# Keys first in self attention, roundings three steps later in cross attention

## The chip, the cores and the metric

The kernel runs on one core of a Trainium2 chip. The metric is the time of one execution on the device in microseconds; lower is better. The core has five engines that run their own instruction streams in order: PE (TensorE), DVE (VectorE), ACT (ScalarE), POOL (GpSimd) and SP (SyncE, which only issues DMA transfers here). They meet at semaphores: an instruction may wait until a semaphore has reached a count, and whatever stands behind it on its engine waits too.

## The reference

Two transformer layers over x (16 batches of 56 tokens, width 256) with a context ctx (16 batches of 1500 tokens, width 256). The change touches the attention part of the second layer:

```python
ln_out = _ln(hidden_states, ln_w, ln_b)
q  = _ln(_fp8_linear_pertensor(ln_out, wq, ...).reshape(b, s, g, hpg, d), qln_w, qln_b)
k  = _ln(_fp8_linear_pertensor(ln_out, wk, ...).reshape(b, s, g, d), kln_w, kln_b)
v  = _fp8_linear_pertensor(ln_out, wv, ...).reshape(b, s, g, d)
core = _gqa(q, k, v)                       # self attention, 56 keys
qx = _ln(_fp8_linear_pertensor(ln_out, wqx, ...), qxln_w, qxln_b)
kx, vx = split(einsum('bsi,oi->bso', cond, w_kv_x))
xout = _gqa(qx, _ln(kx, kxln_w, kxln_b), vx)   # cross attention, 1500 keys
catq = _div_clamp_fp8(concatenate([core, xout]), proj_smooth)
```

There are 16 query heads and 8 key heads of 128 channels. `_div_clamp_fp8` divides, clips to 448 and rounds to bfloat16 and then to fp8.

## The kernel before

Seven stages run one after the other, each with its own block of the five streams: context statistics, attention and experts of the first layer, `self_attention`, `cross_attention`, projection and experts of the second layer. Two of them change.

**`self_attention`** (L727) works on 8 pairs of batches; a pair's 112 tokens lie on the partitions. Its projections are cut into 12 chunks of four heads: queries 0 to 3, queries of cross attention 4 to 7, keys 8 and 9, values 10 and 11 (`KIND`, L716). A turn of a pair has 12 slots, one for each chunk, and each engine's `turn` is a list of what it does in slot t. A chunk is projected by PE (L1016, two slots ahead), squared on ACT (L900), summed on DVE (L1127), made a standard deviation on ACT (L906), normalised on DVE (L1134, L1136), transposed by PE (L1027) and copied by ACT (L933). The attention of the pair before runs in the same slots, at places given by tables (L778 to L780): `SCORES` on PE (L1037, L1040), `MAXIMA` on DVE (L1142, L1146), `EXPS` on ACT, `SUMS` on DVE and POOL, `TURNED` (transposes) and `VALUES` on PE, `OUTPUT` (rounding on DVE L1158 to L1164, then POOL L869, L874). `SCALED` and `QUANTISED` say in which slots the inputs of the next two pairs are rounded. PE's projection takes one of three PSUM banks, so it waits for the normalisation three chunks back.

**`cross_attention`** (L1217) runs over 32 units, two (h = 0, 1) for each batch b, four key heads each; a unit has 6 steps of two context tiles of 125 tokens. Step i of unit u on each engine:
- PE: scores of unit u (L1468, 24 one-pass products of high and low parts), then small work of older units, then the values of the step ten back (L1505, 24 products). The small work: step 0 transposes of the maxima (L1514), step 1 and 2 the folding of the next unit's queries (L1445), step 2 spreading the maximum (L1475) and the sums of the exponentials of unit u-2 (L1528), step 4 spreading their reciprocals (L1480), step 5 the value projection (L1489).
- DVE: scores times scale (L1556), minus the maximum (L1574), low part of the exponentials (L1580), running maximum (L1593, L1598), and for unit u-3 in step 0 the scaled result ca (L1561) and its rounding cb, ce, cc (L1602 to L1606).
- ACT: exponential (L1422), high part (L1427), in step 3 the diagonal of reciprocals (L1404) and the copy ut (L1410), in step 4 rsc (L1417).
- POOL: sum of the exponentials (L1355, L1358, L1361), low part of the context (L1366, in steps 1, 3 and 5 of h = 1), and the end of the rounding of unit u-3 (L1370, L1374), which writes `cat`.
- SP: its queue of one batch is shown below. `load_ct(b, c)` brings chunk c (of three) of the transposed context's high and low parts, which PE needs from step 2c of the first unit of b on (L1459). `store` waits for `cat_ready`.

```python
for c in range(NCH):
    load_cn(b, c)
if more:
    load_q(b + 1)
if not first(b):
    store(b - 1, 0)
if more:
    load_ct(b + 1, 0)
    load_ct(b + 1, 1)
if not first(b):
    store(b - 1, 1)
if more:
    load_ct(b + 1, 2)
```

`load_ct(b + 1, c)` itself waits for the scores of step 2c + 1 of the second unit of b.

## Time and profile before

| | |
|---|---|
| median of 3 runs | 2896.24 us (2894.05 to 2896.83) |
| the profiled execution | 2896.9 us, of it 2895.1 us from first to last instruction |
| PE, PE weight load | 2545.1 us (88%), 2221.3 us (77%) |
| DVE, ACT, POOL | 2156.1 us (74%), 1100.6 us (38%), 928.2 us (32%) |
| mean granted TensorE clock | 0.940 |
| self attention (first projection to last rounding) | 1050 to 1397 us |
| cross attention | 1404 to 2650 us |
| DMA | 231.89 MB, mean 80 GB/s |

The shares are means over seven stages, each limited by something else. How a stage is limited is read from its own stretch: the busy share of each engine and the granted clock there, then which wait comes before which instruction. A time stands for the start of an instruction, counted from the start of the span; the number behind it is its duration. In square brackets stands the idle time of the engine before the instruction, and what ended it; "issue" is idle time for which no releaser was found.

### The profile page before, as it was taken

What the parts mean: (1) busy time and instruction counts of PE and PEld (TensorE: products, weight loads), DVE (VectorE), ACT (ScalarE), POOL (GpSimd) and SP (SyncE); (2) the same over time, 40 slices, a digit from 0 to 9 for tenths busy, and PEclk for the clock granted to TensorE, in tenths of its full rate; (3) what the DMA queues carried; (4) which work ended last, traced back from release to release, by engine and by line L of the source; (5) the groups of instructions that cost most, each with busy time, mean ns of one, the idle gap of its engine ahead of it and who ended that gap; (6) DMA issues with size and microseconds to landing.
All of it is one profiled execution on the core that took longest, in us unless ns stands there. A gap on an engine that the chain in (4) does not pass through costs nothing. (4 is left out here: it accounts for less than half of the span.)

```text
span 2895.1 us, 39559 instructions
## 1 busy us (share of the span) xinstructions
PE 2545.1 (88%) x13434; PEld 2221.3 (77%) x13434; DVE 2156.1 (74%) x3892; ACT 1100.6 (38%) x1787; POOL 928.2 (32%) x584
## 2 busy tenths in 40 slices
PE   7999999939999957777699999999999999986797
PEld 5777777738999945666588888888888888875797
DVE  8777777773333367777488889999999999993377
ACT  1000000014444445556144444545444444444332
POOL 6560000000000012443255555555555555553000
PEclk9999999969999958888799999999999999998899
DMA  6444333120111030101322122222222222213311
GB/s 240 182 172 158 137 143 135 55 73 30 59 44 44 0 115 26 39 39 39 118 73 70 62 73 73 73 73 71 70 66 68 69 69 65 65 38 86 103 50 40
DMA packets 116412, 231.89 MB, mean 80 GB/s; under 512 B 22176, under 2 KB 94704, under 8 KB 112240
## 3 DMA queue, kind: packets, MB, share of 16 engines
q1 hardware_dynamic: 112880, 218.35, 22.2%
q0 software_dynamic: 3456, 12.58, 1.1%
q8 instruction: 40, 0.66, 0.1%
q14 instruction: 36, 0.29, 0.0%
HBM read 158.95 MB, written 71.96 MB: 80 GB/s over the span
## 5 line engine op out<-in xcount | busy, mean ns | idle before, releaser
L1358 POOL TENSOR_TENSOR s_acc<-s_acc,s_sx 125x896 f32<-125x896 f32 x128 | 356.4, 2784 | 249.0 <-ACT s_sx L1422 248.9
L290 DVE BATCH_NORM_STATS2 s_st<-ps 125x6 f32<-125x128 f32 x1536 | 316.2, 286 | 114.2 <-PE ps L246 112.4
L1422 ACT ACTIVATE s_sx<-s_sx 125x896 f32<-125x896 f32 x192 | 184.0, 959 | 461.4 <-DVE s_sx L1574 461.3
L1505 PE MATMUL ps<-s_p_hi,s_cn_hi 125*128 125x448 f32 x768 | 297.7, 388 | 7.3 <-DVE s_p_lo L1580 6.9
L1468 PE MATMUL ps<-s_qc_hi,s_ct_hi 128*125 128x448 f32 x768 | 294.5, 383 | 1.3 <-issue 1.3
L1556 DVE TENSOR_TENSOR s_sx<-ps,keep_krs 125x896 f32<-125x896 f32 x192 | 208.7, 1087 | 106.8 <-PE ps L1468 103.2
L1468 PE MATMUL ps<-s_qc_lo,s_ct_hi 128*125 128x448 f32 x768 | 286.0, 372 | 0.0
L1468 PE MATMUL ps<-s_qc_hi,s_ct_lo 128*125 128x448 f32 x768 | 285.4, 372 | 0.0
L1505 PE MATMUL ps<-s_p_lo,s_cn_hi 125*128 125x448 f32 x768 | 283.1, 369 | 0.0
L1505 PE MATMUL ps<-s_p_hi,s_cn_lo 125*128 125x448 f32 x768 | 282.8, 368 | 0.0
L246 PE MATMUL ps<-s_wk_hi,s_hi 128*125 128x512 f32 x768 | 246.5, 402 | 40.3 <-DVE s_st L290 21.8
L1580 DVE TENSOR_TENSOR s_p_lo<-s_sx,s_p_hi 125x896 fp32r<-125x896 f32 x192 | 264.3, 1377 | 4.9 <-ACT s_p_hi L1427 4.9
L845 POOL MEMSET s_mask<- 112x112 f32 x1 | 0.2, 185 | 794.9 <-POOLq L432 794.9
L246 PE MATMUL ps<-s_wk_hi,s_lo 128*125 128x512 f32 x768 | 243.3, 398 | 0.0
L246 PE MATMUL ps<-s_wk_lo,s_hi 128*125 128x512 f32 x768 | 243.3, 398 | 0.0
L666 DVE TENSOR_TENSOR s_g_lo<-s_g,s_g_hi 128x898 fp32r<-128x898 f32 x64 | 70.1, 1096 | 214.4 <-ACT s_g_hi L495 214.4
L229 ACT ACTIVATE s_hi<-s_raw 128x3000 fp32r<-128x3000 f32 x16 | 43.4, 2714 | 470.4 <-PE ps L246 466.3
L1574 DVE TENSOR_TENSOR s_sx<-s_sx,ps 125x896 f32<-125x896 f32 x192 | 206.4, 1075 | 1.1
L246 PEld LDWEIGHTS ps<-s_wk_hi,s_hi 128*125 128x125 f32 x768 | 143.3, 188 | 82.1 <-DVE s_st L290 28.4
L1593 DVE TENSOR_TENSOR s_mxh<-s_mxh,s_sx 125x896 f32<-125x896 f32 x128 | 197.7, 1545 | 0.1
L1427 ACT ACTIVATE s_p_hi<-s_sx 125x896 fp32r<-125x896 f32 x192 | 183.1, 954 | 11.3 <-DVE s_p_lo L1580 4.3
L246 PEld LDWEIGHTS ps<-s_wk_lo,s_hi 128*125 128x125 f32 x768 | 144.9, 189 | 37.3
(303 smaller groups left out, 6054.9 us busy)
## 6 DMA issues: line engine op xcount, KB each, us to landing
s_raw<-in_ctxt SPq DMA_DIRECT2D x16, 1500.0 KB, 7.3
ct_hi<-s_hi SPq DMA_DIRECT2D x16, 1500.0 KB, 10.4
ct_lo<-s_lo SPq DMA_DIRECT2D x16, 1500.0 KB, 13.6
s_ct_hi<-ct_hi SPq DMA_DIRECT2D x48, 500.0 KB, 3.8
s_ct_lo<-ct_lo SPq DMA_DIRECT2D x48, 500.0 KB, 4.5
s_cn_raw<-in_ctx SPq DMA_DIRECT2D x48, 500.0 KB
s_w<-in_w SPq DMA_DIRECT2D x16, 1024.0 KB, 5.3
qx<-s_qxs SPq DMA_DIRECT2D x16, 448.0 KB, 2.8
```

Source lines behind the costliest of these rows:

```text
L246: mm = pe.matmul(kx[0:TT, t % NB, h, :], a[:, k, TT * t:TT * t + TT], w[:, k, 512 * h:512 * h + 512], start=(n == 0), stop=(n == 5))
L290: ins = dve.bn_stats(st[:, G * t + g, :], kx[0:TT, t % NB, g // 4, DH * (g % 4):DH * (g % 4) + DH])
L666: dve.tensor_tensor(g_lo[r][:, :], g32[r][:, :], g_hi[r][:, :].bitcast(F32), ALU.subtract).then_inc(s["g_lo_ready"], 1)
L1358: pool.tensor_tensor(a, a, p[:, PR * w.pt:PR * w.pt + PR, :], ALU.add).then_inc(s["acc_ready"], 1)
L1422: act.activation(p, p, ACT.Exp).then_inc(s["exp_ready"], 1)
L1427: act.activation(p_hi[w.pr][:, :, :], p, ACT.Copy).then_inc(s["hi_ready"], 1)
L1468: mm = pe.matmul(sc[st % 2][:, j, :], a[:, k, at:at + TT], x[w.h][:, k, :], start=(c == 0), stop=(c == 5))
L1505: mm = pe.matmul(pv[:, k, :], x[:, t, k * P:k * P + P], y[w.vr][:, j, :], start=(t == 0 and c == 0), stop=(t == NT - 1 and c == 2))
L1556: dve.tensor_tensor(by_group(sx[w.h][:, tiles, :]), by_group(sc[st % 2]), krs_b[:, tiles, HG * w.h:HG * w.h + HG].unsqueeze(3).to_broadcas ...
L1574: dve.tensor_tensor(p, p, mb.unsqueeze(1).to_broadcast([TT, PR, QH]), ALU.subtract).then_inc(s["sub_ready"], 1)
L1580: dve.tensor_tensor(p_lo[w.lr][:, :, :], p, p_hi[w.lr][:, :, :].bitcast(F32), ALU.subtract).then_inc(s["lo_ready"], 1)
L1593: dve.tensor_tensor(mxh[:, :, :], a, sx[w.h][:, tiles, :], ALU.max).then_inc(s["mxh_ready"], 1)
```

## The change

Self attention: the chunks are taken in another order, keys, queries, queries of cross attention, values (`ORDER`). With the keys there at the start, the scores and maxima of a pair run in its own turn (slots 7 to 11), and exponentials, sums, transposes, values and outputs in slots 0 to 7 of the next turn, the last output in slot 0 of the turn after that. The rounding of the inputs has new slots; that of the values' input is done inside the loop and no longer ahead of it.

Cross attention: PE's sums L1528 move from the end of step 2 to step 3, between scores and values, and wait for the next unit's second low part of the queries too, which DVE now makes first in step 3. ca of unit u-2 is made in step 5 of unit u, cb, ce, cc and POOL's part of unit u-3 in step 3 and not in step 0. The reciprocals are split into a high and a low part on DVE, ACT makes two diagonals (eight instructions, not four), and PE spreads them with two one-pass products in place of one product in full float32. SP's stream has no line in the diff.

The core of the diff:

```diff
-LAST = [NQ - 1, 2 * NQ - 1, 2 * NQ + NK - 1, CHUNKS - 1]
-KIND = [0] * NQ + [1] * NQ + [2] * NK + [3] * NK
+PART = [0] * NQ + [1] * NQ + [2] * NK + [3] * NK
+TURN_OF = [2, 0, 1, 3]
+ORDER = [c for part in TURN_OF for c in range(CHUNKS) if PART[c] == part]
+KIND = [TURN_OF.index(PART[c]) for c in ORDER]
+LAST = [max(c for c in range(CHUNKS) if KIND[c] == kind) for kind in range(4)]
...
-        SCORES, MAXIMA, EXPS = (0, 1, 2, 3), (1, 2, 3, 4), (5, 5, 5, 5)
-        SUMS, TURNED, VALUES, OUTPUT = (6, 7, 7, 8), (8, 9, 10, 11), (9, 10, 11, CHUNKS), (10, 11, CHUNKS, CHUNKS + 5)
-        SCALED, QUANTISED = ({}, {7: 0, 9: 1, 10: 2, 11: 3}), ({0: 3}, {8: 0, 10: 1, 11: 2})
+        SCORES, MAXIMA, EXPS = (7, 8, 9, 10), (8, 9, 10, 11), (CHUNKS,) * 4
+        SUMS, TURNED = [tuple(CHUNKS + t for t in ts) for ts in ((1, 2, 2, 3), (3, 4, 5, 6))]
+        VALUES, OUTPUT = [tuple(CHUNKS + t for t in ts) for ts in ((4, 5, 6, 7), (5, 6, 7, CHUNKS))]
+        SCALED, QUANTISED = ({3: 3}, {3: 0, 9: 1, 10: 2}), ({4: 3}, {4: 0, 10: 1, 11: 2})
...
-                    if a == 0:
-                        pe.wait_ge(s["tr_read"], NORMED * q + NORMED)
+                    pe.wait_ge(s["tr_read"], NORMED * q + NK + a + 1)
...
@@ cross attention: steps_of
-            act(B + 1, 0)
+            act(B + 1, 3)
@@ POOL
-                    if w.i == 0 and w.three_back:
+                    if w.i == 3 and w.three_back:
                         d = w.u - 3
                         pool.wait_ge(s["cc_ready"], d + 1)
@@ ACT
-                        act.wait_ge(s["r4_ready"], w.u - 1)
+                        act.wait_ge(s["r4_lo_ready"], w.u - 1)
...
-                        for j in range(HG):
-                            ins = act.activation(rdiag[:, j, :], keep.ident[0:PAIR, 0:PAIR], ACT.Copy, scale=r4[:, j:j + 1])
+                        for part, r in enumerate((r4_hi[:, :].bitcast(F32), r4_lo[:, :])):
+                            for j in range(HG):
+                                ins = act.activation(rdiag[part][:, j, :], keep.ident[0:PAIR, 0:PAIR], ACT.Copy, scale=r[:, j:j + 1])
@@ PE
+                    if w.i == 3 and w.two_back:
+                        pe.wait_ge(s["acc_ready"], NPR * (w.u - 1))
+                        if w.one_back:
+                            pe.wait_ge(s["mt_read"], w.u)
+                        if w.new and w.next:
+                            pe.wait_ge(s["qc_lo_ready"], K2 * w.u + 2 * K2)
+                        for j in range(HG):
+                            mm = pe.matmul(sums[:, j:j + 1], acc[w.h][:, 0, PAIR * j:PAIR * j + PAIR], keep.ones[0:TT, 0:1], start=True, stop=True)
+                        mm.then_inc(s["sum_ready"], 1)
                     if w.i == 4 and w.two_back:
                         pe.wait_ge(s["rdiag_ready"], w.u - 1)
-                        if w.new and w.next:
-                            pe.wait_ge(s["qc_lo_ready"], K2 * w.u + 2 * K2)
-                        pe.matmul(misc[:, 0:QH], keep.ones[0:PAIR, :], rdiag[:, :, :], start=True, stop=True).then_inc(s["rb_ready"], 1)
+                        for part in range(2):
+                            mm = pe.matmul(misc[:, 0:QH], ones_r[:, :], rdiag[part][:, :, :], start=(part == 0), stop=(part == 1))
+                        mm.then_inc(s["rb_ready"], 1)
...
-                    if w.i == 2 and w.two_back:
-
-                        pe.wait_ge(s["acc_ready"], NPR * (w.u - 1))
-                        if w.one_back:
-                            pe.wait_ge(s["mt_read"], w.u)
-                        for j in range(HG):
-                            mm = pe.matmul(sums[:, j:j + 1], acc[w.h][:, 0, PAIR * j:PAIR * j + PAIR], keep.ones[0:TT, 0:1], start=True, stop=True)
-                        mm.then_inc(s["sum_ready"], 1)
@@ DVE
+                    if w.i == 3 and w.next and w.new:
+                        qc_split(w.u + 1, 1 - w.h, 1)
...
-                    if w.i == 0 and w.three_back:
-                        dve.wait_ge(s["rb_read"], w.u - 2)
-                        dve.wait_ge(s["v_ready"], w.u - 2)
-                        dve.tensor_tensor(ca[:, :], misc[:, 0:QH], rsc[:, :], ALU.mult).then_inc(s["v_read"], 1)
-                        dve.wait_ge(s["v_read"], w.u - 2)
...
                         dve.reciprocal(r4[:, :], sums).then_inc(s["r4_ready"], 1)
+                        dve.wait_ge(s["r4_ready"], w.u - 1)
+                        dve.tensor_copy(r4_hi[:, :], r4[:, :]).then_inc(s["r4_hi_ready"], 1)
+                        dve.wait_ge(s["r4_hi_ready"], w.u - 1)
+                        dve.tensor_tensor(r4_lo[:, :], r4[:, :], r4_hi[:, :].bitcast(F32), ALU.subtract).then_inc(s["r4_lo_ready"], 1)
...
+                    if w.i == NPR - 1 and w.two_back:
+                        dve.wait_ge(s["rb_read"], w.u - 1)
+                        dve.wait_ge(s["v_ready"], w.u - 1)
+                        dve.tensor_tensor(ca[:, :], misc[:, 0:QH], rsc[:, :], ALU.mult).then_inc(s["v_read"], 1)
...
+                    if w.i == 3 and w.three_back:
+                        dve.wait_ge(s["v_read"], w.u - 2)
...
+                        dve.tensor_scalar(cb[:, :], ca[:, :], FP8_MAX, -FP8_MAX, ALU.min, ALU.max).then_inc(s["cb_ready"], 1)
...
-                    if w.i == 0 and w.three_back:
...
-                        dve.tensor_scalar(cb[:, :], ca[:, :], FP8_MAX, -FP8_MAX, ALU.min, ALU.max).then_inc(s["cb_ready"], 1)
```


## Rows read from the trace of the kernel before

**Rows 1.** Stretches of 100 us: busy time of each engine, granted clock, DMA share.

```profile
core 0: us, PE busy (x) PEld busy (x) DVE busy (x) ACT busy (x) POOL busy (x), PEclk, DMA share, GB/s
...
1100.00:1200.00 100.00, 76.68 (x398) 60.05 (x397) 80.21 (x176) 62.50 (x121) 35.88 (x36) 0.84 0.08 29
...
1900.00:2000.00 100.00, 94.30 (x505) 84.98 (x504) 93.12 (x84) 48.30 (x88) 55.38 (x25) 1.00 0.20 63
```

**Rows 2.** PE in order of time: start us, duration us, line, operands.

```profile
1899.56 0.45 PE L1468 MATMUL ps<-s_qc_hi,s_ct_hi 128*125 128x448 f32 x1
...
1904.52 0.37 PE L1468 MATMUL ps<-s_qc_hi,s_ct_hi 128*125 128x448 f32 x1
...
1910.18 0.37 PE L1468 MATMUL ps<-s_qc_hi,s_ct_hi 128*125 128x448 f32 x1
...
1916.88 0.36 PE L1468 MATMUL ps<-s_qc_hi,s_ct_hi 128*125 128x448 f32 x1
...
1936.49 0.92 PE L1528 MATMUL ps<-keep_ones,s_acc 125*112 125x1 f32 x8 [1.42 <-issue]
...
1938.16 0.45 PE L1468 MATMUL ps<-s_qc_hi,s_ct_hi 128*125 128x448 f32 x1
```

**Rows 3.** Waits from 1700 to 2500: us in total, times, longest us.

```profile
PE ps L1528 <- issue: 28.1, 22, 1.5
...
PE ps L1514 <- DVE s_ca L1561: 15.8, 10, 1.6
```

**Rows 4.** SP in order of time; last line: transfers of L1300 to landing.

```profile
1931.40 0.37 SPq L1317 DMA_DIRECT2D cat<-s_cat  x1
...
1932.68 0.56 SPq L1300 DMA_DIRECT2D s_ct_lo<-ct_lo  x1
...
2006.49 0.37 SPq L1317 DMA_DIRECT2D cat<-s_cat  x1
...
DMA to landing us min/median/max: 4.3/4.5/7.4
```

**Rows 5.** DVE, ACT and POOL in order of time in cross attention.

```profile
1898.66 3.27 DVE L1593 TENSOR_TENSOR s_mxh<-s_mxh,s_sx 125x896 f32<-125x896 f32 x1
...
1902.48 1.09 DVE L1556 TENSOR_TENSOR s_sx<-ps,keep_krs 125x896 f32<-125x896 f32 x1 [0.54 <-PE ps L1468]
...
1904.02 0.17 DVE L1569 RECIPROCAL s_r<-ps 112x4 f32<-112x4 f32 x1
...
1904.23 1.23 ACT L1404 ACTIVATE s_rdiag<-keep_ident,s_r 112x112 f32<-112x112 f32 x4 [3.85 <-DVE s_r L1569]
...
1905.36 0.90 ACT L1410 ACTIVATE s_ut<-ps 128x896 f32<-128x896 f32 x1
...
1907.17 2.12 POOL L1355 TENSOR_TENSOR s_acc<-s_sx 125x896 f32<-125x896 f32 x1 [6.19 <-ACT s_sx L1422]
...
1909.25 2.41 POOL L1366 TENSOR_TENSOR s_cn_lo<-s_cn_raw,s_cn_hi 125x1024 fp32r<-125x1024 f32 x1
...
1929.02 1.03 POOL L1370 TENSOR_TENSOR s_cs<-s_cb,s_cc 128x448 f32<-128x448 bf16 x1 [0.53 <-DVE s_cc L1606]
```

**Rows 6.** PE after a pause, and a stretch (columns as in Rows 1).

```profile
1404.50 1.83 PE L1445 MATMUL ps<-s_q,keep_wk 128*128 128x112 f32 x7 [14.80 <-DMA s_q<-qx]
...
1411.20:1417.00 5.80, 5.78 (x16) 5.13 (x17) 0.93 (x1) 0.00 (x0) 0.00 (x0) 0.51 0.62 230
```

**Rows 7.** DVE in order of time in self attention.

```profile
1201.74 0.69 DVE L1136 TENSOR_TENSOR s_qn<-ps,s_hrs 112x512 f32<-112x512 f32 x1
...
1216.24 0.69 DVE L1136 TENSOR_TENSOR s_qn<-ps,s_hrs 112x512 f32<-112x512 f32 x1
...
1294.78 0.69 DVE L1136 TENSOR_TENSOR s_qn<-ps,s_hrs 112x512 f32<-112x512 f32 x1
...
1358.81 0.69 DVE L1136 TENSOR_TENSOR s_qn<-ps,s_hrs 112x512 f32<-112x512 f32 x1
...
1369.00 0.62 DVE L1142 TENSOR_REDUCE s_mx<-ps 112x4 f32<-112x448 f32 x1
```

More of the change, by code:

```diff
@@ L785, in self_attention @@
         beyond = lambda p: isinstance(p, int) and p >= NP
-        slots = lambda p: range(max(OUTPUT) + 1 if beyond(p) else CHUNKS)
+        slots = lambda p: range(max(OUTPUT) - CHUNKS + 1 if beyond(p) else CHUNKS)
         def at_slot(table, t, p, act):
             for a in range(NQ):
-                if table[a] == t and not early(p, 1):
-                    act(p - 1, a)
-                elif table[a] == t + CHUNKS and not early(p, 2):
-                    act(p - 2, a)
+                back, left = divmod(table[a] - t, CHUNKS)
+                if left == 0 and back >= 0 and not early(p, back) and not beyond(p - back if isinstance(p, int) else p):
+                    act(p - back, a)
         def input_work(table, t, i, r, act):
-            if t in table[r] and not (isinstance(i, int) and (i >= COUPLES or i == 0 and r == 0 or i == COUPLES - 1 and r == 1)):
+            if t in table[r] and not (isinstance(i, int) and i + r >= COUPLES):
                 act(i + r, table[r][t])
@@ L880, in turn @@
                         input_work(QUANTISED, t, i, par, round_input)
-                for kind in range(4):
+                for kind in range(3):
                     round_input(0, kind)
@@ L921, in spread @@
                         if not early(p, 1):
-                            act.wait_ge(s["scores_ready"], NQ * (p - 1) + c + 1)
-                        out, wt, bs = qt[:, QC * c:QC * c + QC, :], keep.col("qln_w"), keep.col("qln_b")
+                            act.wait_ge(s["scores_ready"], NQ * p)
+                        out, wt, bs = kt[:, QC * c:QC * c + QC, :], keep.col("kln_w"), keep.col("kln_b")
                     elif KIND[c] == 1:
-                        if c == NQ and not early(p, 1):
+                        q = c - NK
+                        out, wt, bs = qt[:, QC * q:QC * q + QC, :], keep.col("qln_w"), keep.col("qln_b")
+                    else:
+                        q = c - NK - NQ
+                        if q == 0 and not early(p, 1):
                             act.wait_ge(s["qx_stored"], 32 * p)
-                        q = c - NQ
                         out, wt, bs = qxs[:, :, QC * q:QC * q + QC, :].rearrange("p b h s -> p h b s"), qxw[:, 0:1], qxb[:, 0:1]
                         src = src.rearrange("p h (b s) -> p h b s", b=2)
-                    else:
-                        q = c - 2 * NQ
-                        out, wt, bs = kt[:, QC * q:QC * q + QC, :], keep.col("kln_w"), keep.col("kln_b")
                     act.activation(out, src, ACT.Identity, bias=bs, scale=wt).then_inc(s["tr_read"], 1)
-                    if c == 2 * NQ - 1:
+                    if c == NORMED - 1:
                         act.wait_ge(s["tr_read"], NORMED * p + c + 1)
@@ L959, in turn @@
                         live = not beyond(p)
-                        if live and t < NORMED and t != EXPS[0] + 1:
+                        if live and t < NORMED and t != EXPS[0] - CHUNKS + 1:
                             std_of(p, t)
@@ L966, in turn @@
                             weight_hi(t + AHEAD)
-                        if early(p, 1) and t == 9:
+                        if early(p, 1) and t == 5:
                             act.wait_ge(s["wk_psum"], 1)
@@ L977, in turn @@
                         input_work(SCALED, t, i, par, scale_input)
-                        if live and t == EXPS[0]:
+                        if live and t == EXPS[0] - CHUNKS:
                             std_of(p, t + 1)
@@ L989, in _ @@
                 act.wait_ge(s["yt_ready"], K2)
-                for kind in range(4):
+                for kind in range(3):
                     scale_input(0, kind)
@@ L1073, in turn @@
                         at_slot(TURNED, t, p, turn_probs)
-                        at_slot(VALUES, t, p, lambda q, a: values(q, a, 1 - par if VALUES[a] == t else par))
-                        if early(p, 1) and t == 8:
+                        at_slot(VALUES, t, p, lambda q, a: values(q, a, 1 - par))
+                        if early(p, 1) and t == 4:
                             pe.wait_ge(s["wk_loaded"], 16)
@@ L1193, in _ @@
                     weight_lo(c)
-                for kind in range(1, 4):
+                for kind in range(1, 3):
                     quantise(0, kind)
@@ L1557, in run @@
                                           krs_b[:, tiles, HG * w.h:HG * w.h + HG].unsqueeze(3).to_broadcast([TT, PR, HG, PAIR]), ALU.mult).then_inc(s["sc_read"], 1)
-                    if w.i == 0 and w.three_back:
-                        dve.wait_ge(s["rb_read"], w.u - 2)
-                        dve.wait_ge(s["v_ready"], w.u - 2)
-                        dve.tensor_tensor(ca[:, :], misc[:, 0:QH], rsc[:, :], ALU.mult).then_inc(s["v_read"], 1)
-                        dve.wait_ge(s["v_read"], w.u - 2)
-                    if w.i in (2, 3) and w.next and w.new:
-                        qc_split(w.u + 1, 1 - w.h, w.i - 2)
+                    if w.i == 2 and w.next and w.new:
+                        qc_split(w.u + 1, 1 - w.h, 0)
                     if w.i == 3 and w.two_back:
```

33 lines of the change are left out of this document (17 added, 16 removed).

## The prediction

> **What bounds the kernel now.** I read first the stretches of 100 us, to see what each stage waits for. In self attention (1050 to 1397 us) no engine is full: DVE is busiest with 80% of the time [rows 1], so the order of the work sets the pace there. In cross attention (1404 to 2650 us, over 40% of the span) PE is busy 94% at granted clock 1.00, DVE 93% [rows 1]. So PE sets the pace of cross attention, with DVE close behind. The waits of that stage tell where PE still stands: before the sums of L1528, 28.1 us in 22 units, and before the transposes of L1514, 15.8 us in the same 800 us [rows 3]. DVE has 7% of its time left [rows 1], some slack, though little.
>
> Then PE in order of time gives the length of each step [rows 2]. I name a step by its index i (0 to 5) within a unit, and S3 is the moment at which the scores of step 3 begin. A batch b is two units, h = 0 and h = 1. Step 3 lasts 1904.52 - 1899.56 = 4.96 us, step 4 5.66 us. From S3 to the next unit's S0 it is 17.32 us. A batch takes 2006.49 - 1931.40 = 75.1 us [rows 4].
>
> Last, the queue of SP, since the change moves a producer (the rounding) whose store stands in that queue. SP waits in order. Its body b is: loads of the context, load of q, store(b-1, 0), load_ct(b+1, 0), load_ct(b+1, 1), store(b-1, 1), load_ct(b+1, 2). Now store(b-1, 1) goes at 1931.40, its POOL instruction L1370 having begun at 1929.02 [rows 4, 5]. The last load of ct behind it is issued at 1932.68 and lands 4.5 us later (median) at 1937.2 [rows 4]. PE wants that part at step 4 of the same unit, at 1938.16 + 4.96 = 1943.1 [rows 2]. That is 5.9 us of slack.
>
> **The rounding moves three steps, and SP's loads with it.** Unit d is rounded in unit d+3. Before that was in step 0, after it is in step 3, on DVE (cb, ce, cc) and on POOL (cs, cat). The diff leaves SP's order alone. So for every b from 1 to 14, load_ct(b+1, 2) now stands behind a store that is ready only after step 3 of unit 2(b+1), and PE needs this load at step 4 of that very unit. I follow the new chain from S3 (h = 0), each length read from rows 5 unless another group is named:
> - the product of scores and scales starts on DVE 1902.48 - 1899.56 = 2.9 us after S3, and takes 1.0 us: 3.9;
> - reciprocal, high part, low part: the reciprocal takes 0.17 us, each waits for the one before it. No row has the other two; between 0.17 and 0.7 us together, I take 0.5, as each is as small as the reciprocal and pays one handover. With the handover to ACT: 4.6;
> - ACT spreads the reciprocals eight times, not four. Four took 1905.36 - 1904.23 = 1.13 us, so 2.26: 6.9;
> - ACT copies ut, then the exponential, and POOL may start its sum 1907.17 - 1905.36 = 1.81 us later: 8.7. The rounding on DVE, queued behind three of its instructions of about 1 us, is done by then;
> - POOL's sum stands ahead of cs in POOL's order, 2.12 us: 10.8;
> - from the start of cs to SP's store 1931.40 - 1929.02 = 2.38 us [rows 4, 5]: 13.2;
> - from the store to the issue of ct_lo 1.28 us, 4.5 us to land [rows 4]: 19.0.
>
> PE is ready for step 4 after 4.96 us and the sums of L1528, which now stand in step 3 (0.8 us of their 0.92, the rest overlaps [rows 2]): 5.8. So PE stands 13.2 us in each such batch (bounds 12 and 15).
>
> The other store, store(b-1, 0), moves likewise to step 3 of the unit with h = 1, and load_ct(b+1, 0) behind it is wanted at S0 of the next unit. The chain is the same to 10.8. Then POOL has the low part of the context ahead of cs (h = 1 alone), 2.41 us and up to 1 us more when DVE takes its turn: 13.7. Then 2.38, 1.28 and 4.5: 21.9. PE arrives after 17.32 + 0.8 (L1528) - 0.3 (below) = 17.8. It stands 4.1 us (bounds 2 and 6.5).
>
> After a pause the granted clock is low. After the 14.8 us pause and short starts at this stage's beginning 16 matmuls took 5.8 us at granted clock 0.51 [rows 6], the lower level of 1.2 GHz, where the 24 matmuls of step 3 at the full level take 4.96/24 = 0.207 us each [rows 2]. That is 5.8 - 16 x 0.207 = 2.5 us lost. I take 2.5 us for the long stall, and for the short one 1.2, half way between nothing and 2.5: 3.7 per batch.
>
> Sum of the harm: 14 x (13.2 + 4.1 + 3.7) = 294 us.
>
> **What cross attention gains.** The sums of L1528 go from step 2 to behind the scores of step 3, more than 2.4 us later than the 1.42 us wait [rows 2] asks for, and V is scaled (L1561) in step 5, not in the next step 0, so L1514 no longer waits for it. Gain per batch: 2 x 28.1/22 + 15.8/10.65 = 4.0 us (800 us hold 10.65 batches [rows 3, 4]), and 0.5 as my estimate for PE's refill after each wait. The spread of reciprocals costs PE 5.66 - 4.96 = 0.70 us [rows 2]; two one-pass products like those at 0.207 us cost 0.41. That is 0.3 a unit, 0.6 a batch. ACT's 1.13 us more per unit and DVE's 0.5 lie beside PE's work, apart from the chain above; if that cover went they would cost 32 x 0.5 = 16 us on DVE. The new wait on qc_lo ahead of the sums queues the values of step 3 behind it; DVE makes this part first in step 3, before the scores are ready, so 0 (0.6 us a unit at worst). Gain: 16 x 5.1 = 82 us.
>
> Where V's scaling now stands it comes ahead of two maxima in DVE's step 5. A maximum (L1593) begun while POOL worked took 3.27 us [rows 5]. By the Trainium skill ("SBUF — State Buffer", section on the two separate sides) DVE with two SBUF inputs and POOL lock a shared port pair for a whole instruction. By that rule mx_ready may come 1 to 3 us later, and the wait at L1514 would stay: 82 would become 82 - 16 x 1.5 = 58. In my forecast the stalls let DVE run ahead, so I keep 82; the difference lies inside the range.
>
> **Self attention.** Keys go first, so a pair's scores run in slots 7 to 10 of its own turn, where slots 10 and 11 had only roundings and waits. Two pairs take 1294.78 - 1216.24 = 78.5 us [rows 7]. Of these, 14.5 us go from one normalisation to the next across the turn's end (slot 9 of an odd pair at 1201.74, slot 0 at 1216.24 [rows 7]), with roundings of outputs and inputs by turns on DVE and POOL. After, the output roundings stand in slots 5, 6, 7 and 0, the first input rounding in slot 4, and three of the four maxima come in. DVE's own 80% bounds the gain at 0.2 x 78.5 = 15.7 us for two pairs; the other bound is a loss of 5, as PE gets transposes, values and scores in the same slots 4 to 7. I take a gain of 8: over the seven intervals 28 us. At the end the last pair's maxima began 10.2 us after its last normalisation (1358.81 to 1369.00 [rows 7]), queued behind the former pair's output; now they begin before it: 8 us. Together 36 us (bounds -15 and 65).
>
> **The sum** against the profiled execution, 2896.9 us: + 294 - 82 - 36 = 3073. The median of the runs is 0.7 us lower, so 3072.
>
> **The rivals.**
> 1. SP's loads don't hold PE up (I misread the order, or a wait elsewhere lets them go). Then only the gains stand: 2896.2 - 82 - 36 = 2778, faster. For it speaks that now the same queue costs nothing; against it that the slack is 5.9 us and cat moves 1929.0 to about S3 + 10.8 = 1949, 20 us. Chance 0.06.
> 2. Only the long stall is there, the short one is covered (POOL or the DMA is 4 us quicker). 3072 - 14 x (4.1 + 1.2) = 2998. Chance 0.12.
> 3. The clock stays low longer, as the stalls come twice in each batch and each lowers it: three times the loss, 3072 + 14 x 7.4 = 3176. The row speaks of one pause; nothing shows two in turn. Chance 0.10.
>
> **How the numbers follow.** Forecast 0.70, rivals 0.06, 0.12 and 0.10, and 0.02 for anything near no change. The forecast's own bounds are 14 x (12 + 2 + 1) = 210 less 147 for the best, 14 x (15 + 6.5 + 5) = 371 less 43 for the worst, seldom all at once; I take 3010 to 3150. The range reaches down to rival 2 and leaves out rivals 1 and 3: 2985 to 3150. Faster by over 0.2% 0.07, within 0.2% (what a measurement of this kernel can tell) 0.01, slower 0.92.
>
> **What would show it.** In the changed kernel's waits PE's scores wait for the DMA into ct: 14 times some 13 us, 14 times some 4 us. SP's own waits show store after store waiting for cat; ct_lo is issued some 14 us after S3, not 6 us before it. A batch takes 75.1 + 21.0 - 5.1 = 91 us. The waits of L1528 and L1514 are gone. Two pairs in self attention take about 71 us. The first unit in which PE waits is number 4 (batch 2). Wrong would be: no wait on ct's DMA, a wait of one size only, or a granted clock of 1.00 through the stage.

## The result, and the profile of the changed kernel

The changed kernel takes 3090.48 us (median of 4 runs, 3085.96 to 3101.55), the kernel before 2895.79 us in the same comparison: ratio 1.0679, 95% interval 1.065 to 1.0707. It is slower by 195 us. The forecast was 3072 us with a range of 2985 to 3150. The profiled execution took 3089.54 us against 2896.9 before, so 192.6 us have to be accounted for:

| stretch, by PE's instructions | before, us | after, us | difference |
|---|---|---|---|
| up to the first fold of cross attention | 1404.5 | 1372.4 | -32.1 |
| from there to the last value projection | 1240.3 | 1465.3 | +225.0 |
| the rest of the span | 250.3 | 250.0 | -0.3 |

All of the loss lies in cross attention. The same stretches of 100 us as in [rows 1], columns as there:

```profile
core 0: us, PE busy (x) PEld busy (x) DVE busy (x) ACT busy (x) POOL busy (x), PEclk, DMA share, GB/s
1100.00:1200.00 100.00, 81.36 (x453) 64.58 (x452) 80.02 (x191) 64.93 (x132) 44.90 (x45) 0.88 0.08 29
1900.00:2000.00 100.00, 73.73 (x382) 66.66 (x382) 65.03 (x68) 39.00 (x74) 42.95 (x22) 0.88 0.19 62
```

In self attention DVE is busy for the same 80% as before but gets through 191 instructions where it got through 176. In cross attention PE falls from 94% to 74%, DVE from 93% to 65%, and the granted clock from 1.00 to 0.88. No engine has become the bound: they all stand and wait for something else. The waits of PE and of SP's queue from 1700 to 2500 us (us in total, times, longest us), to be held against [rows 3], say for what:

```profile
PE ps L1472 <- DMA s_ct_lo<-ct_lo: 152.9, 17, 13.2
PE ps L1487 <- DVE s_qc_lo L1546: 6.9, 18, 0.6
...
SPq L1320 <- POOL s_cat L1377: 629.0, 17, 40.4
```

L1472 are the scores (L1468 before), L1487 the sums (L1528 before), L1320 the store of the rounded output. That SP's store waits for POOL is nothing new (545.6 us in 22 in the kernel before, the longest 27.6); that PE waits for a load is. PE waits for a load, the load stands behind a store, the store waits for POOL's rounding. One long stall in order of time, with the chain that ends it. The step begins at 1982.48 (S3 of a unit with h = 0):

```profile
1982.48 0.45 PE L1472 MATMUL ps<-s_qc_hi,s_ct_hi 128*125 128x448 f32 x1
...
1985.40 1.09 DVE L1563 TENSOR_TENSOR s_sx<-ps,keep_krs 125x896 f32<-125x896 f32 x1
1986.41 0.17 DVE L1571 RECIPROCAL s_r<-ps 112x4 f32<-112x4 f32 x1
...
1986.82 0.17 DVE L1575 TENSOR_TENSOR s_r_lo<-s_r,s_r_hi 112x4 f32<-112x4 f32 x1
...
1987.10 1.23 ACT L1408 ACTIVATE s_rdiag<-keep_ident,s_r_hi 112x112 fp32r<-112x112 f32 x4 [2.45 <-DVE s_r_lo L1575]
1988.24 1.21 ACT L1408 ACTIVATE s_rdiag<-keep_ident,s_r_lo 112x112 fp32r<-112x112 f32 x4
...
1991.16 2.07 POOL L1358 TENSOR_TENSOR s_acc<-s_sx 125x896 f32<-125x896 f32 x1 [10.15 <-ACT s_sx L1426]
1993.20 1.02 POOL L1373 TENSOR_TENSOR s_cs<-s_cb,s_cc 128x448 f32<-128x448 bf16 x1
...
1995.56 0.37 SPq L1320 DMA_DIRECT2D cat<-s_cat  x1
...
1996.83 0.56 SPq L1303 DMA_DIRECT2D s_ct_lo<-ct_lo  x1
...
2001.63 0.73 PE L1472 MATMUL ps<-s_qc_hi,s_ct_hi 128*125 128x448 f32 x1 [12.73 <-DMA s_ct_lo<-ct_lo]
2002.16 0.57 PE L1472 MATMUL ps<-s_qc_lo,s_ct_hi 128*125 128x448 f32 x1
...
2005.43 0.37 PE L1472 MATMUL ps<-s_qc_lo,s_ct_hi 128*125 128x448 f32 x1
```

Counted from S3: scale 2.9 us, ACT 4.6, POOL's sum 8.7, cs 10.7, store 13.1, ct_lo issued 14.35, PE goes on at 19.15. The forecast had 2.9, 4.6, 8.7, 10.8, 13.2, 14.5 and 19.0. The last three lines show the price of the pause beyond its own length: the matmuls after it take 0.57 us instead of 0.37 us, started 0.37 instead of 0.2 us apart, until the one at 2005.43. The granted clock of that stretch is 0.50, the 1.2 GHz level (columns as in [rows 1]):

```profile
2001.70:2004.90 3.20, 3.20 (x9) 2.83 (x10) 0.00 (x0) 0.00 (x0) 0.00 (x0) 0.50 0.34 116
```

The short stall, in the other unit of the same batch (S3 at 1940.49):

```profile
1951.51 2.42 POOL L1369 TENSOR_TENSOR s_cn_lo<-s_cn_raw,s_cn_hi 125x1024 fp32r<-125x1024 f32 x1
1953.88 1.90 POOL L1373 TENSOR_TENSOR s_cs<-s_cb,s_cc 128x448 f32<-128x448 bf16 x1
...
1957.80 0.38 SPq L1320 DMA_DIRECT2D cat<-s_cat  x1
...
1959.12 0.55 SPq L1303 DMA_DIRECT2D s_ct_lo<-ct_lo  x1
...
1963.86 0.46 PE L1472 MATMUL ps<-s_qc_hi,s_ct_hi 128*125 128x448 f32 x1 [4.57 <-DMA s_ct_lo<-ct_lo]
```

Over the stage there are 14 long stalls (12.5 to 13.2 us, mean 12.8) and 14 short ones (4.3 to 5.1, mean 4.6), the first in batch 2. After them PE runs 8 to 11 matmuls at the lower clock, by their number some 1.6 us lost after a long stall and 1.5 after a short one. So the stalls cost 14 x (12.8 + 4.6 + 3.1) = 286 us. As the stage grew by 225, the rest of the change brought it 61 us; this is what is left over, not a reading of its own. A batch takes 92.1 us (75.1 before, [rows 4]).

Self attention: the same step of two pairs, 71.7 us apart (78.5 in [rows 7]), and at the end the last pair's first maximum, now ahead of its last normalisation (10.2 us behind it in [rows 7]):

```profile
1217.35 0.69 DVE L1138 TENSOR_TENSOR s_qn<-ps,s_hrs 112x512 f32<-112x512 f32 x1
...
1289.04 0.69 DVE L1138 TENSOR_TENSOR s_qn<-ps,s_hrs 112x512 f32<-112x512 f32 x1
...
1335.88 0.61 DVE L1144 TENSOR_REDUCE s_mx<-ps 112x4 f32<-112x448 f32 x1
1337.34 0.69 DVE L1138 TENSOR_TENSOR s_qn<-ps,s_hrs 112x512 f32<-112x512 f32 x1
```

### The profile page after: what moved, and what is told of

Its sections match the earlier page's. It is cut to its first block and busy times, and to the rows that moved or that the text cites. A ratio compares the mean times of both kernels' runs of the same rounds, so it can differ in the third digit from the quotient of the medians.

```text
span 3087.7 us, 39783 instructions
## 1 busy us (share of the span) xinstructions
PE 2559.0 (83%) x13434; PEld 2238.4 (72%) x13434; DVE 2079.8 (67%) x3956; ACT 1132.2 (37%) x1915; POOL 907.1 (29%) x584
## 5 line engine op out<-in xcount | busy, mean ns | idle before, releaser
L1472 PE MATMUL ps<-s_qc_hi,s_ct_hi 128*125 128x448 f32 x768 | 312.4, 407 | 245.2 <-DMA s_ct_lo<-ct_lo 239.3
L1361 POOL TENSOR_TENSOR s_acc<-s_acc,s_sx 125x896 f32<-125x896 f32 x128 | 319.5, 2496 | 487.1 <-ACT s_sx L1426 484.7
L1472 PEld LDWEIGHTS ps<-s_qc_hi,s_ct_hi 128*125 128x125 f32 x768 | 156.2, 203 | 270.4 <-issue 242.8
L1472 PE MATMUL ps<-s_qc_lo,s_ct_hi 128*125 128x448 f32 x768 | 300.6, 391 | 0.0
L1472 PE MATMUL ps<-s_qc_hi,s_ct_lo 128*125 128x448 f32 x768 | 299.5, 390 | 0.0
L1518 PE MATMUL ps<-s_p_hi,s_cn_hi 125*128 125x448 f32 x768 | 289.3, 377 | 5.2 <-DVE s_p_lo L1586 4.4
```

Source lines behind the costliest of these rows:

```text
L1361: pool.tensor_tensor(a, a, p[:, PR * w.pt:PR * w.pt + PR, :], ALU.add).then_inc(s["acc_ready"], 1)
L1472: mm = pe.matmul(sc[st % 2][:, j, :], a[:, k, at:at + TT], x[w.h][:, k, :], start=(c == 0), stop=(c == 5))
L1518: mm = pe.matmul(pv[:, k, :], x[:, t, k * P:k * P + P], y[w.vr][:, j, :], start=(t == 0 and c == 0), stop=(t == NT - 1 and c == 2))
```

## The experiments

The questions were three: are the stalls the store's place in SP's queue and nothing else; how much is each part worth alone; and, as the first answers came in, why cross attention gains less than the waits of [rows 3] promised. All ratios are against the kernel before in the same comparison. The rows of PE's waits are from 1700 to 2500 us (total us, times, longest us), the stretch of [rows 3].

**1. Both stores behind the loads that follow them.** The changed kernel with another order of SP's queue:

```diff
-                    if not first(b):
-                        store(b - 1, 0)
+                    if not (static(b) and b < 2):
+                        store(b - 2, 1)
                     if more:
                         load_ct(b + 1, 0)
                         load_ct(b + 1, 1)
                     if not first(b):
-                        store(b - 1, 1)
+                        store(b - 1, 0)
                     if more:
                         load_ct(b + 1, 2)
...
```

> The changed kernel with SP's queue reordered alone: in batch b the store of the second unit of b-2 goes ahead of the loads of ct, the store of the first unit of b-1 between chunks 1 and 2, so that no load of ct stands behind a store that is made later than PE needs the load. Theory (loads held behind stores): both waits of PE on the DMA into ct go, 14 x (12.8 + 4.6) = 243 us, and with them the slow clock behind each, 14 x 3.1 = 43 us, so 3090 - 286 = 2804 us. Rival (the eight reciprocal instructions on ACT or DVE's added work is what costs, and the DMA wait only shows it): at least half of the loss stays, 2990 us or more.

Measured: 2846.31 us (2842.72 to 2848.03), ratio 0.9823 (0.9807 to 0.984). No wait for a load of ct is left, and 244 us come back. So the stalls were the order of SP's queue. But 2804 was expected, and 42 us are missing. PE's waits show where:

```profile
PE ps L1528 <- DVE s_mx L1618: 23.9, 11, 2.2
PE ps L1488 <- DVE s_qc_lo L1547: 8.2, 21, 0.6
```

The wait before the transposes (L1528 here), which should have gone with the move of V's scaling, is there under another name: 23.9 us against the 15.8 of [rows 3], now for the maximum that follows that scaling in DVE's step 5. After ten of the eleven 2.2 us waits 6 to 9 matmuls run at the lower clock (granted clock 0.98 over the 800 us).

**2. Only one store moved behind.** Both stores stand ahead of the loads of ct, in the order store(b - 2, 1), store(b - 1, 0), load_ct 0, 1, 2.

> The changed kernel with only the long stall's store moved (the store of the second unit ahead of the first loads of the next batch's body); the store of the first unit stays ahead of chunk 0. Theory (two separate stalls, each of its own store): the 12.8 us waits go and the 4.6 us waits stay, 3090 - 14 x (12.8 + 1.5) = 2890 us. Rival (one stall only shifts into the other): the 4.6 us waits grow and the time stays above 3000 us.

Measured: 2893.22 us (2887.91 to 2894.76), ratio 0.9984 (0.9975 to 0.9994), as expected to 3 us. The long stalls are gone, the short ones stay, and it is the short ones' size:

```profile
PE ps L1473 <- DMA s_ct_lo<-ct_lo: 47.3, 10, 4.9
```

The two stalls are two stores, each with its own load behind it. The difference to experiment 1 is only 46.9 us, 3.3 a batch, where a short stall with its slow clock counts 4.7 + 1.5 = 6.2: with the stall gone, waits on DVE take about half of its place, as the rows of experiment 1 show.

**3. The rounding back in step 0, SP's order as it was.**

```diff
-            act(B + 1, 3)
+            act(B + 1, 0)
...
-                    if w.i == 3 and w.three_back:
+                    if w.i == 0 and w.three_back:
...
```

The last edit stands twice, on POOL and on DVE.

> The changed kernel with the rounding (cb, ce, cc, cs, cat) back in step 0, SP's order as it was. Theory: cat is ready as early as in the kernel before, no wait on ct is left, and all gains of the change stand, 2896 - 32 (self attention) - 82 (cross attention) = 2782 to 2810 us. Rival (the lock between DVE and POOL makes the maxima late where V's scaling now stands ahead of them): PE waits again at the transposes of the maxima, and the time is 2815 us or more.

Measured: 2890.79 us (2884.07 to 2898.44), ratio 0.9978 (0.9966 to 0.9991). No wait for ct here either, which confirms the cause from the other side. But the theory that all gains stand (2782 to 2810) fell, and the rival held:

```profile
PE ps L1487 <- DVE s_qc_lo L1546: 26.5, 21, 2.0
PE ps L1527 <- DVE s_mx L1617: 19.4, 10, 2.6
```

That is 45.9 us, as much as the 43.9 of [rows 3], and 3.3 us more before the values, at granted clock 0.96 instead of 1.00. The old waits are gone and equal ones have come in their place. In the changed kernel itself this was hidden: its DVE is busy 70% of the 800 us (560.68 us), 90% here (720.38), and its waits have no line for the transposes.

One thing speaks for the rounding in step 3. Its second instruction, ce, takes 2.08 us in step 0 (here as in the kernel before), where a sum of POOL's is under way, and 0.28 us in step 3 of the changed kernel. First the kernel before, then the changed one:

```profile
1926.55 2.08 DVE L1604 TENSOR_SCALAR s_ce<-s_cb 128x448 uint16<-128x448 uint16 x1
...
1989.33 0.28 DVE L1602 TENSOR_SCALAR s_ce<-s_cb 128x448 uint16<-128x448 uint16 x1
```

With the rounding in step 3 the wait on the low part of the queries is 8.2 us (experiment 1), not 26.5. How much of the difference hangs on these 1.8 us was not tested.

**4. The new self attention with the old cross attention.** The function of cross attention is the one of the kernel before.

> The new self attention with the cross attention of the kernel before. The two traces put cross attention's first product at 1404.5 us before and 1372.4 after, so 2896 - 32 = 2864 us. Rival (the stage that follows gives part of it back through queries of cross attention that are stored later): 2875 us or more.

Measured: 2861.88 us (2859.53 to 2862.95), ratio 0.9876 (0.986 to 0.9893). Self attention brings some 35 us by itself, so of the some 50 us by which experiment 1 beats the kernel before, only 2861.9 - 2846.3 = 15.6 belong to the new cross attention: 1.0 us a batch on average. In the middle of the stage it is less, 0.2 us: a batch takes 75.1 us here and 74.9 in experiment 1. The rest lies in the first batches (78.0 and 76.7 us for the second and third here, 74.9 there) and at the end of the stage.

**5. The kernel before with only the rounding moved to step 3** (cb, ce and cc on DVE, cs and cat on POOL).

> The kernel before with one part of the change alone: cb, ce, cc, cs and cat at step 3 and not at step 0; V's scaling, the sums and the one product of the reciprocals stay. Theory (loads of ct behind stores): chain from S3 to ct landed 17.9 us with PE ready at 5.0, so 12.9 us, and 20.8 against 17.3, so 3.5 us, slow clock 3.1 us: 14 x 19.5 = 273 us, less some 30 us of waits at the transposes that the stalls cover: 2896 + 243 = 3139 us (3110 to 3160). Rival (the split or the sums are needed for the loss): under 3000 us.

Measured: 3148.19 us (3145.74 to 3150.11), ratio 1.0864 (1.0846 to 1.0882). This one edit makes the whole harm, some 250 us, in a kernel without any of the others; 3139 was expected.

**6. Experiment 1 with one fp32 product of the reciprocals** in place of the two one-pass products of high and low parts, so four copies on ACT and not eight, and no split on DVE.

```diff
-                        for part, r in enumerate((r4_hi[:, :].bitcast(F32), r4_lo[:, :])):
-                            for j in range(HG):
-                                ins = act.activation(rdiag[part][:, j, :], keep.ident[0:PAIR, 0:PAIR], ACT.Copy, scale=r[:, j:j + 1])
+                        for j in range(HG):
+                            ins = act.activation(rdiag_f[:, j, :], keep.ident[0:PAIR, 0:PAIR], ACT.Copy, scale=r4[:, j:j + 1])
...
-                        for part in range(2):
-                            mm = pe.matmul(misc[:, 0:QH], ones_r[:, :], rdiag[part][:, :, :], start=(part == 0), stop=(part == 1))
+                        mm = pe.matmul(misc[:, 0:QH], keep.ones[0:PAIR, :], rdiag_f[:, :, :], start=True, stop=True)
```

> The version with both stores behind the loads (2846 us), and the reciprocals spread again by one product in full float32 from one diagonal. Theory (PE sets the pace, the split saves it 0.3 us a unit): 10 us slower, 2856 us. Rival (DVE and ACT set it, and the three small instructions and four more activations cost more than they save PE): 5 to 15 us faster, 2831 to 2841 us.

Measured: 2825.49 us (2820.96 to 2826.0), ratio 0.9754 (0.9738 to 0.977). The split was to save 0.6 us a batch on PE, yet without it the kernel is 21 us faster, more than the rival's 5 to 15. PE's wait before the transposes is shorter:

```profile
PE ps L1526 <- DVE s_mx L1612: 17.7, 11, 1.7
```

and at 1.62 us it is followed by no slow matmul, where the 2.2 us of experiment 1 was: the granted clock of the stretch is 1.00, not 0.98, and a batch takes 73.4 us, not 74.9. Counted from the sums of the same unit (h = 1), PE arrives at the transposes after 20.5 us with the split and 20.8 us without: the split saves its 0.3 us. But the maximum is ready after 22.53 us with it and 22.25 without. So in both kernels PE waits for the maximum, and the saving only makes the wait longer: PE arrives 0.3 us earlier, the maximum comes 0.3 us later, and a wait of 1.6 us becomes one of 2.2. A batch is 1.5 us shorter without the split. Of this the later maximum is 0.3 us; the rest, some 1.2 us, goes with the matmuls at the lower clock behind the longer wait. ACT's four further copies last 1.2 us, but the maximum is delayed by the 0.3 alone.

What makes the maximum late can be read from DVE and POOL in step 5 of a unit with h = 1 (start us, duration us):

```profile
1789.17 2.78 POOL L1362 TENSOR_TENSOR s_acc<-s_acc,s_sx 125x896 f32<-125x896 f32 x1 [0.16 <-ACT s_sx L1426]
1790.43 2.48 DVE L1607 TENSOR_TENSOR s_mxh<-s_mxh,s_sx 125x896 f32<-125x896 f32 x1
1791.92 3.22 POOL L1370 TENSOR_TENSOR s_cn_lo<-s_cn_raw,s_cn_hi 125x1024 fp32r<-125x1024 f32 x1
1792.94 2.68 DVE L1612 TENSOR_TENSOR s_mx<-s_mxh 125x448 f32<-125x448 f32 x1
1795.75 0.42 PE L1526 MATMUL ps<-keep_ident,s_mx 125*112 125x125 f32 x2 [1.62 <-DVE s_mx L1612]
```

Each of the three behind POOL's sum ends after the other engine's by nearly as long as it takes alone (1.08 us for a maximum of 896 columns, 2.40 for the low part, 0.63 for a maximum of 448). The first maximum waits for POOL's sum (end 1791.95) and ends 0.96 us later; POOL's low part of the context then waits for that maximum (end 1792.91) and ends 2.23 us later; the last maximum waits for that (end 1795.14) and ends 0.48 us later. These instructions take turns, never side by side. This is the rule of the Trainium skill, "SBUF — State Buffer", section on the two separate sides: with two SBUF inputs on DVE and a POOL instruction that reads SBUF, the second one is blocked until the first has finished. By that rule, the trace agrees: a 0.6 us instruction that stands behind a 2.2 us one of POOL costs 2.68 us. Not all of DVE's instructions take turns with POOL's: those that read an operand from PSUM (scores times scale, and minus the maximum) take their 1.08 us beside POOL as they do alone, over 60 of each in the 800 us.

**7. The kernel before with only the sums moved to step 3** (and with them the low part of the queries ahead of that step's scaling on DVE).

> The kernel before with another part alone: the sums in step 3, with the second low part of the queries first in DVE's step 3. Theory (the waits before the sums, 2.6 us of a batch, go and nothing takes their place): 2896 - 41 = 2855 us. Rival (the wait moves to the next meeting of PE and DVE, the transposes or the values): 2875 us or more.

Measured: 2908.0 us (2903.82 to 2914.78), ratio 1.0039 (1.0025 to 1.0053), where 2855 was expected. A clear miss. In the kernel before, the wait at the sums ends with POOL's last sum, though [rows 3] names no releaser: in all 22 cases that sum ends 0.1 us before PE goes on. Here the one before the sums at 1936.49 of [rows 2]:

```profile
1935.26 1.14 POOL L1361 TENSOR_TENSOR s_acc<-s_acc 125x448 f32<-125x448 f32 x1
```

Moved, the sums no longer wait for POOL but for the low part of the queries. This wait came with the edit: it stood in step 4 before, where PE had no wait, and now stands in step 3. PE's waits:

```profile
PE ps L1483 <- DVE s_qc_lo L1540: 30.6, 21, 2.4
PE ps L1521 <- DVE s_ca L1562: 8.1, 10, 1.0
```

30.6 us stand where [rows 3] has 28.1, and the granted clock is 0.97. Moving a consumer later helps only if what stands second in time is not just as late.

**8. Experiment 1 with the rounding in step 2** (DVE and POOL), to take it out of POOL's full step.

> The version with both stores behind the loads (2846 us), and the rounding in step 2, where POOL is idle in both units of a batch. Its trace has POOL's low part of the context, cs, cat and two sums in a row in steps 3 to 5 of h = 1, and DVE's maxima of step 5 locked out by them, which makes PE wait 2.2 us at the transposes, with a slow clock behind it. Theory (that row of POOL instructions is what eats the gain): both go, 16 x (2.3 + 1.6) = 62 us, 2784 us. Rival (DVE has too much work in any order): 2825 us or more.

Measured: 2873.92 us (2869.83 to 2878.13), ratio 0.9925 (0.9909 to 0.9942), where 2784 was expected. The wait on the low part of the queries came back (21.2 us in 21), and the one before the transposes stayed (21.3 in 10), at clock 0.97. So taking the rounding out of POOL's full step does not bring the gain back. Of the three places tried for the rounding (steps 0, 2 and 3), none is free of waits on DVE; which instruction makes them late in step 2 was not traced.

**9. Experiment 6 with POOL's low part of the context cut to 8 columns of each tile.** Three such instructions run in each batch. The rest of the low part stays zero, so this kernel leaves out a part of the computation.

```diff
-                        pool.tensor_tensor(cn_lo[:, at, :], cn_raw[c][:, :, :], cn_hi[:, at, :].bitcast(F32), ALU.subtract)
+                        pool.tensor_tensor(cn_lo[:, at, 0:8], cn_raw[c][:, :, 0:8], cn_hi[:, at, 0:8].bitcast(F32), ALU.subtract)
```

> This is the kernel with both stores behind the loads and one fp32 product of the reciprocals (2825.5 us), with the low part of the context computed on POOL for 8 of its columns only; the rest of it is zero, so this leaves out that part of the computation (a shorter POOL instruction, three times in a batch), and nothing else. Theory (DVE is late for the last maximum because POOL's 3.22 us instruction on the low part of the context and DVE lock each other out): the last maximum takes well under its 2.68 us and the PE wait before the transposes, 1.62 us in each batch (17.7 us in 11 batches), is gone: 2825 - 16 x 1.6 = 2799, 2790 to 2805. Rival (DVE has too much work in this step whatever POOL does, or POOL's sum takes the place of the low part): at least 1 us of the 1.62 stays, 2815 or more.

Measured: 2783.26 us (2781.24 to 2784.42), ratio 0.9613 (0.9597 to 0.9629). Nothing on PE or DVE was touched, and PE's waits are gone: 5 us in 800, PE busy for 794.9 us of them, a batch 70.9 us. The gain is 42 us, more than the 26 of the one wait, as the 0.8 us a batch on the low part of the queries went too. DVE's last maximum (mean ns behind the bar), in experiment 6 and here:

```profile
L1612 DVE TENSOR_TENSOR s_mx<-s_mxh 125x448 f32<-125x448 f32 x22 | 36.3, 1651 | 0.8
```

```profile
L1615 DVE TENSOR_TENSOR s_mx<-s_mxh 125x448 f32<-125x448 f32 x23 | 14.4, 625 | 0.8
```

The same instruction on the same data takes 625 ns when POOL is out of its way. In experiment 6 the 1651 ns are a mean of two kinds: 11 with h = 0 take 0.63 us, 11 with h = 1 take 2.68. This settles that POOL's instruction, and not the amount of DVE's work, makes the wait before the transposes in experiment 6.

**10. Experiment 6 with the two last maxima ahead of the low part of p and of V's scaling** in DVE's step 5.

> The kernel with both stores behind the loads and one fp32 product of the reciprocals (2825.5 us), with the two last maxima in DVE's step 5 moved ahead of the low part of p and of the scaling of V. Theory (the wait before the transposes is only the place of the maxima in DVE's queue, and the low part of p has slack): mx is ready 2 to 4 us earlier, the wait of 1.62 us a batch is gone and none takes its place: 2825 - 26 = 2799, 2790 to 2806. Rival (DVE is the bound of this step, so what is moved back is late instead: PE waits before the values for the low part of p or before the queries' low part): 2818 to 2840, with a new wait of 1 us or more in a batch.

Measured: 2902.75 us (2897.74 to 2906.64), ratio 1.0025 (1.0015 to 1.0034): worse than experiment 6 by 77 us, the rival's direction and several times its price.

```profile
PE ps L1517 <- DVE s_p_lo L1594: 43.7, 21, 4.1
```

PE waits up to 4.1 us before the values for the low part of p, and the clock of the stretch is 0.96. What DVE has to deliver in this step is late in both orders; the old one was the better.

**11. Experiment 6 with the low part of the context on DVE**, one step later and at its end, in place of POOL. Nothing is left out.

```diff
-                        pool.tensor_tensor(cn_lo[:, at, :], cn_raw[c][:, :, :], cn_hi[:, at, :].bitcast(F32), ALU.subtract)
...
+                        dve.tensor_tensor(cn_lo[:, at, :], cn_raw[c][:, :, :], cn_hi[:, at, :].bitcast(F32), ALU.subtract)
```

> The kernel with both stores behind the loads and one fp32 product of the reciprocals (2825.5 us), with the low part of the context subtracted on DVE, one step later and at the end of the step, in place of POOL. Nothing is left out. Theory (two-input instructions of POOL and DVE lock each other out, so one on DVE alone costs both less): the instruction takes about 1.2 us on DVE (1.08 us for 896 columns) instead of 2.4 to 3.2 us on POOL, DVE's last maximum is short again, and the PE wait before the transposes is gone: 2783 as with 8 columns, plus up to 1 us a batch: 2783 to 2800. Rival (DVE is full, so 3 more instructions in each batch make it late): the waits stay and new ones come on the low part of p or of the queries: 2815 or more.

Measured: 2813.37 us (2811.45 to 2814.3), ratio 0.9708 (0.9692 to 0.9724). It is the fastest of the kernels that compute everything: 2.9% below the kernel before, 9% below the changed one.

```profile
PE ps L1482 <- DVE s_qc_lo L1540: 7.8, 20, 0.6
PE ps L1521 <- DVE s_mx L1607: 6.6, 11, 0.6
...
L1613 DVE TENSOR_TENSOR s_cn_lo<-s_cn_raw,s_cn_hi 125x1024 fp32r<-125x1024 f32 x33 | 61.0, 1848 | 0.0
```

DVE takes on 1.85 us three times in a batch, and still serves PE better than before: the wait before the transposes falls from 1.62 to 0.6 us. But 2783 to 2800 was expected. The instruction was priced at 1.2 us. A third of them took that (11 of 33, with no POOL instruction beside them), the others up to 3.1 us beside POOL's sums: 1.85 on average.

**12. The same move in experiment 4** (new self attention, old cross attention).

> The new self attention with the old cross attention (2861.9 us), and the same move of the low part of the context from POOL to DVE. Nothing is left out. If the old waits, 4.1 us a batch before the sums and the transposes, come from the lock as well, they go by more than half: 2861.9 - 16 x 2.5 = 2822, 2800 to 2835, and what is left to the kernel with the moved sums, rounding and stores is some 30 us. Rival (the old waits come from the places of the steps alone, and the rounding in step 0 stands in the way of the DVE instruction moved there): 2850 or more.

Measured: 2860.15 us (2854.91 to 2866.07), ratio 0.9873 (0.9854 to 0.9892): no difference to 2861.88. The rival's number held, its reason for half.

```profile
PE ps L1525 <- issue: 28.4, 22, 1.5
PE ps L1502 <- DVE s_p_lo L1577: 4.1, 10, 0.4
...
1700.00:2500.00 800.00, 767.49 (x4068) 693.58 (x4068) 707.56 (x716) 391.19 (x690) 366.68 (x173) 0.98 0.22 71
```

The wait before the transposes, 1.6 us a batch, is gone here too, so that one hung on POOL's instruction in the old cross attention too. But the wait before the sums stayed at 28.4 us, so that one does not hang on this instruction; it ends with POOL's last sum here too. And a granted clock of 0.98 instead of 1.00 took back what the first had brought: behind 8 of the 22 waits before the sums 3 to 7 matmuls run at the lower clock, where experiment 4 has none from 1700 to 2500 us. A batch without them takes 74.0 us, one with them 75.5, against 75.1. So the same move pays 12 us in experiment 6 and nothing here. Which of the differences between the two kernels decides that was not tested.

## Why the prediction came true, and what in it was wrong

**The stalls (294 us; 286 measured).** The mechanism held in all its steps: the order of the queue, two stalls a batch of two sizes, their number, the first batch. Experiments 1, 2, 3 and 5 show it by taking it away as a whole, by half, and from its other end, and by making it alone. The long stall was 12.8 us, not 13.2: PE arrived 6.4 us after S3 and not 5.8, in part because the sums waited 0.2 us for the low part of the queries (0.6 in the other unit), the wait that the sum had at nothing. The short one was 4.6, not 4.1: cs and cat took 1.90 and 1.71 us there and not 1.03 each, as DVE had its turns in between, and PE too arrived 1 us later.

**The clock (3.7 us a batch; 3.1 measured).** The guess of half the loss for the short stall was too low (1.5, not 1.2), that of 2.5 for the long one too high (1.6). The third rival, a clock that stays low, did not come: it recovered within 8 to 11 matmuls every time.

**Self attention (36 us; 32 in the trace, some 35 by experiment 4).** Two pairs gained 6.8 us, not 8. The last normalisation came 21.5 us earlier (1358.81 to 1337.34) where seven intervals were to bring 28; the end brought 10.6, not 8.

**The gains of cross attention (82 us; 61 measured).** This term was mis-sized, and would have been wrong by more if the stalls had not covered it. With the stalls taken away the new cross attention gains 15.6 us (experiments 1 and 4). Three steps of it failed.
- "V is scaled (L1561) in step 5, not in the next step 0, so L1514 no longer waits for it": true of V's scaling, but the wait before the transposes went over to the maxima, 23.9 us in place of 15.8. The prediction named this by the rule on the shared port pair, priced it at 24 us, and kept the full 82 because "the stalls let DVE run ahead". That reason was right for the changed kernel, whose waits show no line for the transposes, but the gain came from the stalls and not from the move.
- The wait on the low part of the queries at nothing: 8.2 us in 21 in experiment 1, up to 30.6 with the sums moved alone (experiment 7). The 28.1 us before the sums did go with their place, since POOL's last sum is done by then, but with the rounding in step 0 the next producer was just as late.
- The split product as a gain of 0.6 us a batch: experiment 6 has it at a loss of 21 us over the stage. PE was not the one that came last at the transposes, so its 0.3 us went into the wait, and ACT's and DVE's added work, priced as lying "beside PE's work", made the maximum 0.3 us later. Most of the loss is the lower clock behind the longer wait, a term that the sum had only for the stalls.

Waits in experiment 1 sum to 32.1 us in the stretch against 43.9 before: 11.8 us in 10.65 batches, 1.1 us a batch. But the batch is only 0.2 us shorter (75.1 to 74.9): the matmuls at the lower clock behind the 2.2 us waits, 6 to 9 a batch, take back most of it. That 16 x 1.1 = 18 comes near the 15.6 measured is chance. The gains of the changed kernel, 61 us, are larger; that its stalls give DVE the time that it lacks fits its waits, and was not tested apart.

Of the 21 us between 82 and 61 in the changed kernel, the waits on the low part of the queries (6.9 us in 18 units, 0.8 us a batch) make 12. The other 9 were not tied to a line; they also hold the error of the 286 us, which rests on counted matmuls.

The total came closer than its terms: the stalls were put 8 us too high, the gains of cross attention 21 and those of self attention 4, so 3072 - 8 + 21 + 4 = 3089. That the first error offset a part of the others is luck.

## What to carry over

When a producer moves later, look first at what stands behind its store in the issuing queue and when that is wanted: here the two stores of a batch, made ready three steps later, held up loads, one of which had 5.9 us of slack, and this cost 250 us by itself. Do not count a wait as gained before naming what is second latest, and do not price DVE's work with two operands in SBUF by its mean duration when POOL works at that time: which of the two stands ahead decides. Do not count a saving on an engine that then only waits longer. Where two instructions on POOL and DVE exclude each other, try the work on one engine; in experiment 11 it took more DVE time and made DVE's results earlier, in experiment 12 it gained nothing.

## What the runs showed of the hardware

- DVE instructions with two SBUF inputs and POOL's ran by turns: 625 ns for a maximum of 448 columns with POOL's instruction shortened, 2.68 us behind a POOL subtraction (experiments 6 and 9). One with a single 16-bit SBUF input did too, 0.28 us alone and 2.08 beside a sum of POOL's (the kernel before). Those with an operand in PSUM kept their 1.08 us beside POOL (experiment 6).
- A pause of PE of 1.62 us in each batch was followed by no slow matmul (granted clock 1.00, experiment 6), one of 2.2 us by 6 to 9 in ten of eleven cases (0.98, experiment 1). Pauses of 4.6 and 12.8 us cost nearly the same afterwards, 1.5 and 1.6 us. But experiment 12 had slow matmuls behind 8 pauses of 1.1 to 1.5 us, and the kernel before did both: from 1500 to 1700 us, in batches of 77 to 78 us, its pauses of 1.1 and 1.5 us were followed by 5 to 9 slow matmuls each; from 1700 to 2500 us, with the same pauses and the same third one of 1.6 us, by none (75.1 us). What decides between these stays open.
- Three further subtractions on DVE in each batch, with DVE already busy 88% of the stretch (707.65 of 800 us in experiment 6), made the kernel 12 us faster.
